# Masking two of four attention heads after the exponential, on GpSimd, in a four-block transformer kernel

## What is computed

```python
x = x + _L0_xattn_ref(_layernorm(x), ctx, mask_all_true, ...)   # 2 heads of 64
x = x + _L0_ffn_ref(_layernorm(x), ...)                         # gated, squared relu
x = x + _L1_xattn_ref(_layernorm(x), ctx, ctx, mask, ...)       # 16 heads of 8
x = x + _L1_ffn_ref(_layernorm(x), ...)                         # 8 experts, top 1
```

```python
scores = jnp.einsum('bhsd,bhtd->bhst', qh, kh) / math.sqrt(D_K)
scores = jnp.where(mask == 0, jnp.float32(-1000000000.0), scores)
attn = jax.nn.softmax(scores, axis=-1)
out = jnp.einsum('bhst,bhtd->bhsd', attn, vh)
```

## Time and profile before

| | us |
|---|---|
| median of 3 runs | 298.65 |
| lowest and highest | 297.97, 302.39 |
| span of the profiled execution, first to last instruction | 296.5 |
| median less span | 2.15 |
| second attention, first to last exponential (start) | 87.5 to 234.4 |

### The profile page before, as it was taken

The page is one execution under the profiler, slowest core; times in us unless marked ns, Lnnn a source line. Parts: engine busy times, 40 slices in busy tenths (PEclk is TensorE's granted clock), DMA queues, the critical chain, the costliest instruction groups (busy, mean ns, idle before and its releaser), DMA issues.

```text
span 296.5 us, 5874 instructions
## 1 busy us (share of the span) xinstructions
PE 258.6 (87%) x2048; PEld 129.6 (44%) x2048; DVE 187.7 (63%) x659; ACT 144.1 (49%) x273; POOL 92.3 (31%) x108
## 2 busy tenths in 40 slices
PE   0799998697598999999998999999999888959991
PEld 0345666365353344444433334332444345625550
DVE  3290966849889767678778568664777146724440
ACT  1178465524045656656466356562576533414440
POOL 2643692603403400003300112000214642577533
PEclk9999999879799999999999799995999999988997
DMA  6990456241464689620004999520101893369500
GB/s 177 410 413 20 123 133 158 53 133 35 108 160 110 149 263 271 147 88 2 0 2 143 308 419 309 135 70 9 38 0 37 302 367 85 100 182 362 181 20 7
DMA packets 20812, 44.69 MB, mean 151 GB/s; under 512 B 1670, under 2 KB 15757, under 8 KB 19824
## 3 DMA queue, kind: packets, MB, share of 16 engines
q1 hardware_dynamic: 9296, 30.63, 32.5%
q10 hardware_dynamic: 9824, 10.00, 12.8%
q0 software_dynamic: 1664, 3.69, 3.5%
HBM read 30.90 MB, written 13.93 MB: 151 GB/s over the span
## 4 chain that ended last, share of the span: by engine, by line
PE 47%; DVE 8%; ACT 7%; issue 4%; DMA 3%; POOL 1%; POOLq 0%; DVEq 0%
PE banks L1310 11%; PE banks L1296 8%; PE banks L1226 7%; PE banks L1291 5%; PE banks L1376 5%; DVE scores_unused L977 4%; ACT p_region L716 4%; ACT q_region L700 3%; PE banks L1091 2%; PE banks L1403 2%; DMA binned_dram<-token_rows,mask_bias 1%; DMA q_region<-binned_dram,mask_bias 1%; PE banks L1097 1%; PE banks L1392 1%; PE banks L1383 1%
## 5 line engine op out<-in xcount | busy, mean ns | idle before, releaser
L977 DVE CUSTOM_DVE_ANT_0 scores_unused<-banks,mask_bias 128x512 bf16<-128x512 f32 x128 | 82.9, 688 | 25.9 <-PE banks L1226 25.1
L716 ACT ACTIVATE p_region<-banks 128x1024 f32<-128x1024 f32 x64 | 65.2, 1021 | 59.7 <-PE banks L1296 59.7
L487 POOL TENSOR_TENSOR ln_rstd<-ln_var_eps,minus_half 128x2 f32<-128x2 f32 x16 | 12.2, 765 | 117.0 <-DVE ln_var_eps L785 117.0
L1226 PE MATMUL banks<-k_region,q_region 80*128 80x512 bf16 x128 | 41.7, 397 | 2.0 <-DVE max L977 1.4
L1296 PE MATMUL banks<-q_region,k_region 80*128 80x256 bf16 x256 | 39.6, 278 | 0.0
L1310 PE MATMUL banks<-p_region,values 128*9 128x256 f32 x512 | 35.9, 403 | 2.3 <-DVE mask_bias L903 2.3
L1296 PEld LDWEIGHTS banks<-q_region,k_region 80*128 80x128 bf16 x256 | 20.0, 98 | 16.6 <-issue 15.0
L1291 PE MATMUL banks<-mask_bias_by_key,ident_bf 64*64 64x512 bf16 x256 | 26.7, 407 | 0.6 <-ACT q_region L700 0.6
L1376 PE MATMUL banks<-k_region,q_region 128*64 x64 | 23.0, 483 | 1.5 <-ACT q_region L747 0.8
L569 POOL DMA_INDIRECT binned_dram<-token_rows,mask_bias x8 | 8.2, 1023 | 51.3 <-issue 51.3
L1377 PE MATMUL banks<-k_region,q_region 128*64 128x352 f32 x64 | 23.0, 483 | 0.0
(11 more groups left out here) (146 smaller groups left out, 439.2 us busy)
## 6 DMA issues: line engine op xcount, KB each, us to landing
binned_dram<-ctx_region ACTq DMA_DIRECT2D x2, 4626.0 KB, 26.5
k_region<-experts_dram SPq DMA_DIRECT2D x17, 544.0 KB, 4.7
k_region<-k_parts_dram SPq DMA_DIRECT2D x4, 1152.0 KB
k_region<-experts_dram SPq DMA_DIRECT2D x1, 3808.0 KB, 19.5
q_region<-q_parts_dram SPq DMA_DIRECT2D x12, 192.0 KB
k_region<-mask1k_dram SPq DMA_DIRECT2D x1, 2048.0 KB, 12.0
k_region<-mask_dram SPq DMA_DIRECT2D x1, 2048.0 KB, 16.2
k_parts_dram<-q_region SPq DMA_DIRECT2D x4, 384.0 KB, 2.8
```

The source lines that it names most:

```text
L716: a.activation(pt[:, u % 2, j, :, :].rearrange("p (c t) q -> p c (t q)", c=2), ps[:, c:c + 2, :], ACT.Exp, scale=float(D1) ** -0.5).then_i ...
L977: return v.tensor_tensor_reduce(out=junk[:, q, :], in0=scores, in1=m1b[:, QT * (u // 4) + q, :], scale=1.0, scalar=-3e38, op0=ALU.add, op1 ...
L1226: return m.matmul(out, qst[0:R, (u * GH + j) * SQ + q * P:(u * GH + j) * SQ + (q + 1) * P], kst[0:R, (u * GH + j) * SK:(u * GH + j + 1) * ...
```

## The change

- For heads 0 and 1 of each unit (`KEPT_BY_POOL`) the mask products on PE are gone. After the exponential POOL multiplies the weights, read as 32-bit integers, with an integer 0 or 1 (`keep_weights`, 128x1024, in place), and `weigh` waits for it.
- For heads 2 and 3 the four 64x64 mask products become two 128x128 products of 512 columns.
- The factors lie in a new tile `keep` of one batch, made by a new DVE job `keep` (128x1024, one per batch): 0 where masked, 1 where not, and for a query without any key 1 everywhere.
- DVE has a new small instruction in `minus_maximum`, waited for: a maximum below -2^31 becomes 0 for heads 0 and 1.
- `fm` of batch 3 moves from (4, 1) to slot 17, in front of the second attention, with `keep` 0.
- All of POOL's side work during the second attention now stands between the products, at the place where `BESIDE1` has it; `rows_in` 0 to 7 are placed by `ROWS_SOON_AT`.
- `q_split_rest` shares the memory of `normed3_T`, with a wait on ACT in front of L657; `some_key` is bf16 and has a place for each batch.

```diff
-EARLY_AT = {... "n2": 7, "fm": 8, "n3": 12, "l2T": 8}
+EARLY_AT = {... "n2": 7, "n3": 12, "l2T": 8}
...
-EARLY0 = beside0(EARLY_AT, {2: [("mix", 0)]})
+EARLY0 = beside0(EARLY_AT, {2: [("mix", 0)], 8: [("fm", 0)], 12: [("fm", 1)], 16: [("fm", 2)], 17: [("fm", 3), ("keep", 0)]})
...
+KEPT_BY_POOL = (0, 1)
...
-ROWS_SOONER = PHASE_STEPS[0]
+ROWS_SOON_AT = {(14, 3): (0, 1), (15, 2): (2, 3, 4), (15, 3): (5, 6, 7)}
...
+            def keep_weights(u, j):
+
+                b = u // 4
+                pool.wait_ge(keep_set, b + 1)
+                pool.wait_ge(exp1, 4 * u + j + 1)
+                wt = pt[:, u % 2, j, :, :].bitcast(I32)
+                g.tensor_tensor(wt, wt, keep, ALU.mult).then_inc(kept, 1)
+
             pool.wait_ge(ids_set, 1)
-            for b in PHASE_BATCHES[0]:
-                inverse_root("s4", b)
-                scatter(b)
-            inverse_root("s4", 2)
-            for s in range(ROWS_SOONER // 2):
-                rows_in(s)
-            scatter(2)
-            for s in range(ROWS_SOONER // 2, ROWS_SOONER):
-                rows_in(s)
+            for u in range(UNITS):
+                for j in range(GH):
+                    for kind, b in BESIDE1.get((u, j), []):
+                        if kind in ("s2", "s3", "s4"):
+                            inverse_root(kind, b)
+                        if kind == "n3":
+                            output_bias(b)
+                        if kind == "pos":
+                            scatter(b)
+                    for n in ROWS_SOON_AT.get((u, j), ()):
+                        rows_in(n)
+                    if j in KEPT_BY_POOL:
+                        keep_weights(u, j)
...
+                if kind == "keep":
+                    if b >= 1:
+                        dve.wait_ge(kept, GROUPS * len(KEPT_BY_POOL) * b)
+                    v.scalar_tensor_tensor(keep, m1kb[:, KT * b:KT * (b + 1), :], 0.0, fq[:, b, :].unsqueeze(1).broadcast_to([P, KT, SQ]),
+                                           ALU.is_lt, ALU.not_equal).then_inc(keep_set, 1)
...
+                alone = mx1[:, par, :, 0:len(KEPT_BY_POOL)]
+                chain(v.scalar_tensor_tensor(alone, alone, -BIG / 2, alone, ALU.is_gt, ALU.mult))
...
-                for c in range(2):
-                    for half in range(2):
-                        r = slice(64 * half, 64 * (half + 1))
-                        o = slice(64 * (half ^ c), 64 * ((half ^ c) + 1))
-                        m.matmul(ps[o, first + c, :], identB[r, r], m1kb[r, b * KT + 2 * c:b * KT + 2 * c + 2, :].rearrange("p t q -> p (t q)"),
+                by_pool = j in KEPT_BY_POOL
+                if not by_pool:
+                    for c in range(2):
+                        m.matmul(ps[:, first + c, :], identB, m1kb[:, b * KT + 2 * c:b * KT + 2 * c + 2, :].rearrange("p t q -> p (t q)"),
                                  start=True, stop=False, skip_group_check=True)
...
-                                        qst[0:R, (u * GH + j) * SQ:(u * GH + j + 1) * SQ], start=False, stop=True, skip_group_check=True)
+                                        qst[0:R, (u * GH + j) * SQ:(u * GH + j + 1) * SQ], start=by_pool, stop=True, skip_group_check=True)
...
                     pe.wait_ge(exp1, 4 * (u + 1))
+                    pe.wait_ge(kept, len(KEPT_BY_POOL) * (u + 1))
```

More of the change, by code:

```diff
@@ L82 @@
 AHEAD = 2
-EARLY_AT = {"Q": 13, "parts": 13, "n0": -7, "q": -5, "k0_": -5, "PV": 5, "kk": 9, "wo": 6, "s2": 6, "n2": 7, "fm": 8, "n3": 12, "l2T": 8}
+EARLY_AT = {"Q": 13, "parts": 13, "n0": -7, "q": -5, "k0_": -5, "PV": 5, "kk": 9, "wo": 6, "s2": 6, "n2": 7, "n3": 12, "l2T": 8}
 LATE_AT = {"k2": 9, "V": 4, "l3T": 12, "s0": -8, "rr": 9, "lnT": -6, "v0_": 2, "vv": 11, "s3": 11, "K": 3}
@@ L106 @@
     (3, 0): [("parts", 2)], (3, 1): [("kk", 3)],
[1 row of a table removed]
[1 row of a table added]
     (5, 0): [("s3", 3)], (5, 1): [("oT", 0), ("n3", 3)], (5, 2): [("l3T", 3)], (5, 3): [("wO", 0)],
     (6, 0): [("s4", 0)], (6, 1): [("Q", 3)],
[1 row of a table removed]
+    (7, 0): [("n4", 0)], (7, 1): [("parts", 3)], (7, 2): [("nT", 0)], (7, 3): [("lg", 0)], (8, 0): [("keep", 2), ("hot", 0)], (8, 1): [("pos", 0)],
     (9, 1): [("oT", 1)], (9, 2): [("wO", 1)], (10, 0): [("s4", 1)], (11, 0): [("n4", 1)], (11, 2): [("nT", 1)],
-    (11, 3): [("lg", 1)], (12, 0): [("hot", 1)], (12, 1): [("pos", 1)],
+    (11, 3): [("lg", 1)], (12, 0): [("keep", 3), ("hot", 1)], (12, 1): [("pos", 1)],
     (13, 1): [("oT", 2)], (13, 2): [("wO", 2)], (13, 3): [("s4", 2)], (14, 0): [("n4", 2)], (14, 2): [("nT", 2), ("tabA", 0), ("tabB", 0)],
@@ L220, in build @@
         m1kb = sb("mask1_bias_by_key", [P, B * KT, SQ], BF16)
+        keep = sb("kept_by_key", [P, KT, SQ], I32)
         v1 = sb("values1", [P, B * KT, H1, VW])
@@ L234, in build @@
         gate = sb("gate", [P, QT, D])
-        fq = sb("some_key", [P, 2, SQ])
+        fq = sb("some_key", [P, B, SQ], BF16)
         ln3T = sb("normed3_T", [P, SQ])
-        q_rest = sb("q_split_rest", [P, SQ])
+        q_rest = ln3T
         q_parts = sb("q_split_parts", [P, SPLIT, SQ], BF16)
```

15 lines of the change are left out of this document (6 added, 9 removed), and 3 rows, old and new, of the table BESIDE1.

## The result

The changed kernel takes 332.58 us (median of 4 runs, 331.54 to 335.99), the kernel before 298.61 beside it. The ratio is 1.1186, with a 95% interval of 1.1117 to 1.1255: 11 to 13% slower. The forecast of 296.2 us was wrong, and its range as well. The profile of the changed kernel is that of the longest of the four executions (span 334.1 us), so its span grew by 37.6 us where the medians differ by 34.0.

A forecast was written before the change was run, and what follows sets the result against it. PE, busy for 258.6 of 296.5 us, was taken as the fullest engine. A 14.1 us saving less costs summed to -2.45, giving a 294.05 span and, with 2.15 around it, 296.2 us; range 290 to 302.5.

The forecast's parts named there:

- DVE beside a busy POOL: DVE instructions reading two SBUF tensors slow down while POOL's product runs: +0.3 us (0 to 2).
- The clock: PE's new and longer waits bring some half clock: +1.5 us, bounds 0 and 8.
- Rival 2: Gaps lower the clock each time, in units 8, 9, 12, 13 and at the end: 302 us; chance 0.15.
- A head without masks: Mask products of heads 0 and 1 leave PE: 0.44 us a head, 14.1 us in all.
- Wide masks: Two 512-column mask products at heads 2 and 3 cost PE 0; if dear, 3.2 us in all.
- rival 1: POOL's product is slow, 4.0 us each, and PE waits for it: 302 to 306 us; chance 0.12.
- The wait for `hot`: At (8, 0) and (12, 0) the saving is not seen, +0.9 us, and `keep` 2 and 3 add 2.4.
- `weigh` 8, 12 and 15: PE waits for POOL's product behind `scatter`, 1.5, 1.4 and 1.25 us: +4.15 together (2.2 to 9.9).
- the forecast's other terms: Saving on PE less work added on DVE: 14.1 less 2.0, 0.6, 0.9, 2.4 plus 0.5.
- Units 0 and 1: DVE bounds the first two units, so their four heads save nothing: +1.8 us.
- The start: DVE has `keep` 0, `fm` 3 and the new small instruction in front; most is absorbed by unit 2: +0.2 us.
- a sign of being wrong: In the new profile, PE waiting for POOL in plain units would show the prediction wrong; no size given.

The follow-up runs named there:

- hold only, fast PE: Changed kernel with heads 0 and 1 unmasked, no wait of `weigh` for POOL, and POOL multiplying the factor tile by another integer tile: 336.27 us, ratio 1.122.
- without products: Changed kernel with POOL's 32 products and the waits for them left out, heads 0 and 1 unmasked: 297.29 us, ratio 0.997.
- masks gone: Kernel before with wide mask products for heads 2 and 3, none for heads 0 and 1, nothing added: ratio 0.974.
- the memset: Changed kernel with each POOL product replaced by a POOL memset of about the same length, same waits: 318.33 us, ratio 1.068.
- all masks on PE: Changed kernel with wide masks on PE for all heads, `weigh` not waiting for POOL, and POOL squaring the factor tile: ratio 1.042.

## Why the prediction was wrong

**The step that failed** is the term "DVE beside a busy POOL", +0.3 us with a bound of 2. With a busy POOL and no wait for it the attention is 29.2 us longer (hold only, fast PE, against without products). The step saw the case in its own row, the pair L791, and then named as the instructions to which it applies only `Q`, `parts` "and a few more, mostly with room". It did not name `minus_maximum`, three small instructions a unit on two SBUF operands or of the TENSOR_SCALAR form. An instruction that takes 0.17 us alone took up to 2.32, until POOL's ended; 45 of them cost 18.5 us of DVE's time, and `hot` and `parts` the other 7.4 of 25.9. They stand behind the row maxima of j = 1, in the stretch in which the products of heads 0 and 1 run, and the row maxima of the next heads are queued behind them, for which PE has only two banks. The Trainium skill (GPSIMD Engine Reference, Key points) says that GpSimd contends with VectorE instructions in a two-port mode and with those of two SBUF inputs. For the second kind the trace agrees: L1016 and L1019 were held (up to 1.98 and 2.32 us), the row maxima with one such input were not (0.69 us). TENSOR_SCALAR and CAST read one tensor and were held as well (2.30 and 2.32 us), which fits the first kind if they ran in such a mode; the trace does not name the mode.

**The clock**, charged with 1.5 us and a bound of 8, failed with it. Length times the clock not granted, summed over the windows, is at most what PE lost by it: 29.9 us in the changed kernel, 5.1 before, 10.2 without products. So up to 25 of the 31.1 us are PE at 1.2 GHz. Of the waits with a window behind them, those of 1.9 us or more stand in or ahead of one with a mean clock of 0.58 to 0.84; those of 1.45 and 1.54 us stand in windows at full clock. The length of the wait does not decide it alone: behind the one of 1.29 us in the first window the clock is at 0.50 from 95 to 103 us. Windows right behind the waits of 3.42 and 1.45 us (the first at 259.16, the second at 159.16):

```profile
259.20:263.00 3.80, 3.80 (x18) 2.72 (x19) 2.40 (x13) 2.30 (x3) 1.09 (x1) 0.50 0.08 9
...
159.20:163.00 3.80, 3.80 (x42) 1.74 (x43) 3.04 (x12) 1.40 (x2) 2.84 (x4) 1.00 0.00 0
```

The waits and their clock were not parted by an experiment. Rival 2 had this mechanism. Of the places that it named, units 8, 9 and 12 (0.60, 0.74 and 0.58) and the end (below) did lose their clock, and unit 13 did not (1.00); units 8, 9 and 12 hold 12 of the 25 us. The rest is in units 1, 3, 4 and 5 above all, behind waits for DVE that it did not have.

**What was right.** A head without masks was to be 0.44 us shorter; it is 0.43 by the spacing (0.45 us for 0.88), and two heads make 0.84 us a unit in the run with the masks gone. Wide masks cost 0. `keep` takes 1.22 us (1.2 forecast). The product takes 2.36 us (2.1 taken), so rival 1 did not come about. The wait for `hot` grew as its terms say, from 1.16 us to 1.60 with two heads without masks and to 2.74 with `keep` in front. `weigh` 8, 12 and 15 waited for POOL, 1.98, 1.54 and 1.42 us, where 1.5, 1.4 and 1.25 were forecast (the row of 1.26 us is a plain unit, of which below):

```profile
196.88 1.90 PE L1328 MATMUL banks<-p_region,values 128*9 128x256 f32 x16 [1.98 <-POOL p_region L583]
...
217.02 1.05 PE L1328 MATMUL banks<-p_region,values 128*9 128x256 f32 x16 [1.26 <-POOL p_region L583]
...
243.40 1.05 PE L1328 MATMUL banks<-p_region,values 128*9 128x256 f32 x16 [1.54 <-POOL p_region L583]
...
274.73 1.91 PE L1328 MATMUL banks<-p_region,values 128*9 128x256 f32 x32 [1.42 <-POOL p_region L583]
```

Two slips of arithmetic stand in that step and change nothing of this: 238.5 less 237.33 is 1.17 us and not 1.25, and with a product of 1.2 us the three waits would sum to 1.45, not 2.2.

**What was mis-sized.** Even without products the forecast's other terms, some 9 us saved, came to about 1. Units 0 and 1 did not just fail to gain 1.8 us, they lost another 3.3 (masks gone), the clock again. The two units with `hot` take 5.1 us more with `keep` in front of it than in the run with the masks gone, where 2.4 was charged: half clock stands behind the longer wait. The start was charged with 0.2 us; the windows begin 1.8 us later in the changed kernel, 3.0 without products and 3.8 with `keep` 0 moved into the attention as well, so the place of `keep` 0 is not the reason, and what is was not tested. Two plain units also waited for POOL (1.45 us and the 1.26 above), where a norm on POOL stands ahead of a product; the prediction had named that as a sign of being wrong.

Behind the attention +0.3 was charged, and 4.7 us came. The first 10.43 us there, now and before:

```profile
259.57:270.00 10.43, 10.43 (x69) 5.35 (x70) 3.67 (x24) 5.33 (x7) 4.49 (x4) 0.59 0.52 187
...
226.69:237.12 10.43, 9.00 (x89) 4.36 (x87) 2.67 (x19) 6.69 (x10) 6.46 (x7) 1.00 0.73 238
```

At most 4.3 of the 4.7 us are the clock behind the wait of 3.42 us, and `weigh` 15's wait of 1.42 us, charged elsewhere, lies here too. The six `rows_in` behind the last product are not the cause in the changed kernel, though they begin at 274.75, 15 us behind the last window, where before they ended at 241.3, as far behind: PE's waits for such transfers are 3.3 us in both, and 4.8 without products, where the part behind the attention is 69.4 us.

**How the loss divides.** Of the 34.9 us that the product costs the attention, a busy POOL for which PE does not wait gives 29.2. From the other side, the memset, which keeps every wait for POOL and takes most of the hold away, still costs 15.0. So taking away the waits brings 5.7 us, and taking away most of the hold 19.9: the hold is the larger part. That the two prices sum to more than 34.9 fits waits and holds that lie over each other, which no run parts. The price of the hold depends on PE's speed: with a fast PE it is 29.2 us, with all masks on PE the like of it is some 8 (13.4 less 5.6, a product of 1.90 us). Part of that difference is the shorter product; that the slower PE leaves DVE room would be the rest, which was not measured apart.

## What to carry to other kernels

Before elementwise work goes to POOL, list every DVE instruction of that stretch by its form, not by its size: each one that reads two tensors from SBUF, and each TENSOR_SCALAR or CAST, may last until POOL's instruction ends, and then price what is queued behind it. Do the same with each wait that the change adds: here PE waited 27 us more for DVE and POOL (31.3 for 4.1), and the clock not granted behind such waits came to as much as 25 us. And try the parts of a change apart: the one that looked neutral, the wide mask products, was 1.1 to 1.5% faster alone, and no kernel of this series that computes the whole result is faster.

## What was not expected of the hardware

- A DVE instruction of eight elements takes up to 2.3 us beside a product on POOL of 2.36 us. One took 3.83 us across two memsets in a row, so it did not get in between them; between the two products from 138.95 us L1016 did end and L1017 begin.
- The kind of POOL instruction decides whom it holds: an integer tensor_tensor held DVE's two-tensor forms, TENSOR_SCALAR and CAST; a memset of about the same length held only the last two (means: `minus_maximum` 1 and 3 at 0.17 us, TENSOR_SCALAR at 0.52, CAST at 1.07 and 1.24).
- An integer product of a tile with itself takes 1.90 us on POOL, of two tiles 2.36 (128x1024).
- The same wait of 1.16 us is followed by a granted clock of 0.50 to 0.56 with 64x64 mask products around it and by 1.00 with 128x128 ones (1.17 us, two chips). With heads 0 and 1 without masks a wait of 1.60 us was followed by full clock once and by a lower one once. What makes the difference was not tried.
